# Spreading the next chunk's leaf work over leaves 8 to 14 of a chunked recurrence

## The reference, cut to what matters

```
def step(S, t):
    q_t, k_t, v_t, a_t, b_t = t
    y = jnp.einsum('bhvk,bhk->bhv', S, k_t)
    err = y - v_t
    S = a_t[..., None] * S - (b_t[..., None] * err)[..., None] * k_t[:, :, None, :]
    o = jnp.einsum('bhvk,bhk->bhv', S, q_t)
    return (S, o)
...
o = (o - mu) * jax.lax.rsqrt(var + LN_EPS) * ln_g + ln_b
o = (o * g).reshape(b, t, H * D)
return o @ Wo
```

## Time and profile before

| | us |
|---|---|
| median of 3 runs | 3453.39 (3451.27 to 3462.71) |
| the profiled execution, device time | 3461.74 |
| its span in the trace | 3460.0 |
| first L982 of chunk 0, of chunk 18, of chunk 19, of chunk 20 | 681.56, 1975.95, 2048.01, 2122.75 |
| mean granted TensorE clock, share of full speed | 0.933 |

### The profile page before, as it was taken

One profiled execution on the slowest core, in us unless ns is written; L12 is line 12 of the kernel. 1 busy time (PEld: TensorE's weight loads), 2 busy tenths in 40 slices (PEclk: granted clock), 3 DMA queues, 4 the chain that ended last, 5 costly groups with the idle time before them and its releaser, 6 DMA issues. The chain is left out here.

```text
span 3460.0 us, 48170 instructions
## 1 busy us (share of the span) xinstructions
PE 3028.8 (88%) x14200; PEld 2149.0 (62%) x14200; DVE 2450.5 (71%) x4820; ACT 1595.4 (46%) x3478; POOL 1265.9 (37%) x1452
## 2 busy tenths in 40 slices
PE   5999999378889888898888988889898898788888
PEld 3555555266777677776677767777677776534454
DVE  5777777388888878888878888888888878332222
ACT  3666666255455544555445554555545545211110
POOL 1757666333344333443334433334333344200000
PEclk9999999699999999999989999999999999889999
DMA  1655556621132211322113221122211220110000
GB/s 66 247 216 231 232 211 252 172 43 37 37 62 40 50 39 38 59 43 50 39 37 57 45 50 39 38 57 45 49 39 38 57 45 19 36 61 19 18 18 18
DMA packets 431891, 255.04 MB, mean 74 GB/s; under 512 B 400080, under 2 KB 414128, under 8 KB 416944
## 3 DMA queue, kind: packets, MB, share of 16 engines
q1 hardware_dynamic: 431680, 252.42, 26.4%
HBM read 147.40 MB, written 104.99 MB: 73 GB/s over the span
## 5 line engine op out<-in xcount | busy, mean ns | idle before, releaser
L245 DVE SCALAR_TENSOR_TENSOR A_acc<-A_psY,A_w,A_acc 128x410 f32<-128x410 f32 (+1 forms) x720 | 419.3, 637 | 156.0 <-ACT A_acc L285 156.0
L768 POOL TENSOR_TENSOR B_WT<-B_WT,B_G 128x128 f32<-128x128 f32 (+2 forms) x224 | 186.6, 833 | 869.1 <-issue 446.9
L1069 ACT ACTIVATE B_WL<-B_psT 128x128 f32<-128x128 f32 (+2 forms) x480 | 150.1, 313 | 654.1 <-PE B_psT L1478 654.1
L345 PE MATMUL A_psY<-A_xT,A_w 128*128 128x413 f32 (+1 forms) x960 | 347.2, 510 | 9.1 <-PE A_psAG L351 7.7
L202 POOL TENSOR_TENSOR A_outs<-A_outs,A_acc 128x410 f32<-128x410 f32 (+1 forms) x240 | 229.4, 988 | 254.3 <-ACT A_outs L293 254.3
L982 DVE TENSOR_TENSOR B_NC<-B_NC,B_psM 128x256 f32<-128x256 f32 x480 | 200.1, 417 | 152.3 <-PE B_psM L1502 104.6
L345 PEld LDWEIGHTS A_psY<-A_xT,A_w 128*128 128x128 f32 x960 | 180.2, 189 | 165.5 <-issue 164.3
L985 DVE TENSOR_REDUCE B_W<-B_NC 128x64 f32<-128x320 f32 x512 | 248.8, 486 | 17.6
L1502 PE MATMUL B_psM<-B_BD,B_WL 128*128 128x128 f32 x1536 | 247.3, 305 | 9.2
L1502 PEld LDWEIGHTS B_psM<-B_BD,B_WL 128*128 128x128 f32 x1536 | 207.6, 207 | 75.5 <-ACT B_WL L1069 74.9
L285 ACT ACTIVATE A_acc<-A_psY,A_w 128x410 f32<-128x410 f32 (+1 forms) x240 | 166.2, 692 | 163.0 <-PE A_psY L345 161.3
(11 more groups left out here) (194 smaller groups left out, 7171.8 us busy)
## 6 DMA issues: line engine op xcount, KB each, us to landing
scr<-A_outs SPq DMA_DIRECT2D x48, 1024.0 KB, 5.5
B_KQ<-scr SPq DMA_DIRECT2D x96, 512.0 KB, 6.5
scr<-A_outag SPq DMA_DIRECT2D x32, 1024.0 KB, 8.1
A_xc<-nbeta SPq DMA_DIRECT2D x18, 1024.0 KB, 8.5
scr<-A_x SPq DMA_DIRECT2D x16, 1024.0 KB, 7.6
B_A<-scr SPq DMA_DIRECT2D x32, 512.0 KB, 4.5
B_C<-scr SPq DMA_DIRECT2D x32, 512.0 KB, 4.6
B_G<-scr SPq DMA_DIRECT2D x32, 512.0 KB, 4.6
```

Source lines behind the costliest of these rows:

```text
L245: nc.vector.scalar_tensor_tensor(a, y, w[:, s, col:col + 1], a, ALU.mult, ALU.add)\
L345: last = nc.tensor.matmul(psY[p][:, y0:y0 + HALO + t1 - t0], wp[:, p, kt, :], xT[:, kt, t0:t1 + HALO], start=kt == 0, stop=kt == KT - 1)
L768: tt(dst, dst, gr, ALU.mult).then_inc(wsc.sem, 1)
L1069: copy = lambda out, in_: nc.scalar.activation(out, in_, ACT.Copy)
```

## The change

The same instructions are issued in another order; two waits of ACT and DVE move with them. Nothing is computed that was not computed before.

- DVE: `decays(g + 1)` is split, its first instruction (L828) goes to leaf 8, the two others stay at leaf 9; `mask_own` of the next chunk moves from leaf 10 to 9, `mask_gram(g, 5)` from 9 to 10, `row_pairs(nxt)` from 12 to 11, `leaf_solution(nxt, ...)` from leaves 13, 14 and the boundary to 12, 13 and 14, `invert` from 12 to 14, `att_sum` from 14 to 15, behind `decay_state`.
- `leaf_solution` is cut into other parts: the third of its 8 instructions goes from part 1 to part 2, the sixth from part 2 to part 3. This holds for the chunk's own second half too (leaves 6 and 7).
- PE: the order of `leaf_jobs` from leaf 8 on. `own` 9 to 8, `gram 5` 8 to 9, `decay 0, 1` 10 to 9, `kk` 11 to 10, `ktok` 13 to 11, `var` 10 to 12, `decay 2, 3` 14 to 13, `wo 0` 12 to 13, `wo 1` 13 to 14 (behind `rstd`).
- ACT follows: `leaf_keys` 8 to 7, `sort_keys` 11 to 9, `pairs_copy` 12 to 11, `squares` 9 to 11, the `ktok` copies 14 to 12, `deviation` 11 to 13, `att_copy` 13 to 14.

```diff
-            8: [("gram", 5)],
-            9: [] if last else [("own", 0, 0), ("own", 0, 1)],
-            10: (out and [("var", 0)] or []) + [("decay", 0), ("decay", 1)],
-            11: [] if last else [("kk", 0, 0), ("kk", 0, 1)],
-            12: ([] if last else [("gram", 0)]) + (wo and [("wo", 0)] or []),
-            13: [("ktok", 0), ("ktok", 1)] + (wo and [("wo", 1)] or []),
-            14: (out and [("rstd", 0), ("rstd", 1)] or []) + [("decay", 2), ("decay", 3)]}
+            8: ([] if last else [("own", 0, 0), ("own", 0, 1)]),
+            9: [("gram", 5)] + [("decay", 0), ("decay", 1)],
+            10: ([] if last else [("kk", 0, 0), ("kk", 0, 1)]),
+            11: [("ktok", 0), ("ktok", 1)],
+            12: (out and [("var", 0)] or []) + ([] if last else [("gram", 0)]),
+            13: [("decay", 2), ("decay", 3)] + (wo and [("wo", 0)] or []),
+            14: (out and [("rstd", 0), ("rstd", 1)] or []) + (wo and [("wo", 1)] or [])}
...
                     step(0, n[:, :, 12:18:5], x02, many(n[:, :, 7:8], 2), ALU.mult)
+                elif part == 2:
                     step(1, n[:, :, 5:16:5], n[:, :, 5:16:5], TMP[:, :, 0:3], ALU.add)
-                elif part == 2:
...
+                else:
                     step(5, rows23, rows23, tmp2, ALU.add)
-                else:
...
+                    elif j == 8 and more:
+                        decays(g + 1, (0,))
                     elif j == 9:
                         if more:
-                            decays(g + 1)
+                            decays(g + 1, (1,))
+                            mask_own(g + 1, 0, 0)
+                            mask_own(g + 1, 0, 1)
+                    elif j == 10:
                         mask_gram(g, 5)
...
                     elif j == 11:
+                        if more:
+                            row_pairs(nxt)
                         decay_state(g, 0)
                         decay_state(g, 1)
                     elif j == 12:
+                        if more:
+                            leaf_solution(nxt, 1)
+                    elif j == 13:
+                        if more:
+                            leaf_solution(nxt, 2)
+                        if more:
+                            mask_gram(g, 0)
+                    elif j == 14:
+                        if more:
+                            leaf_solution(nxt, 3)
                         if g:
                             invert(g - 1)
...
                         decay_state(g, 2)
                         decay_state(g, 3)
+                        if g % 2 and g >= 3:
+                            att_sum((g - 3) // 2)
...
                     add_state(g, i)
-                if more:
-                    leaf_solution(nxt, 3)
```

More of the change, by code:

```diff
@@ L817, in _, with decays @@
             wait(dve, zeros, 0, NZERO)
-            def decays(g):
+            def decays(g, parts=(0, 1)):
                 s = g % 2
@@ L827, in decays @@
                 a, e = by_leaf_row(A[:, s]), E[:, s]
[L828 to L832, removed]
+                if 0 in parts:
+                    tt(e[:, F_ + 1:B_ + 2:3], a[:, 0:3], a[:, 1:4], ALU.mult).then_inc(dec.sem, 1)
+                if 1 in parts:
+                    wait(dve, dec, g, 1)
+                    tt(e[:, F_ + 2:B_ + 1:4], e[:, F_ + 1:RR_ + 1:3], a[:, 2:4], ALU.mult).then_inc(dec.sem, 1)
+                    wait(dve, dec, g, 2)
+                    tt(e[:, F_ + 3], e[:, F_ + 2], a[:, 3], ALU.mult).then_inc(dec.sem, 1)
             def coefs(h):
@@ L1014, in chunk @@
                         leaf_solution(here, 3)
+                    elif j == 8 and more:
+                        decays(g + 1, (0,))
                     elif j == 9:
                         if more:
-                            decays(g + 1)
+                            decays(g + 1, (1,))
+                            mask_own(g + 1, 0, 0)
+                            mask_own(g + 1, 0, 1)
+                    elif j == 10:
                         mask_gram(g, 5)
-                    elif j == 10 and more:
-                        mask_own(g + 1, 0, 0)
-                        mask_own(g + 1, 0, 1)
                     elif j == 11:
+                        if more:
+                            row_pairs(nxt)
                         decay_state(g, 0)
@@ L1151, in pairs_copy, with key_tokens @@
                 copy(X[:, 0:3:2, :], ps[:, 0:4 * HJ2].rearrange("p (k x) -> p k x", k=4)[:, 0:3:2]).then_inc(nlc.sem, 1)
+            def key_tokens(g, i):
+                ps = take_bank(act, g, "ktok", i)
+                wait(act, stu, g, 0)
+                copy(KTOK[:, 4 * i:4 * i + 4, :].rearrange("p n c -> p (n c)"), ps[:]).then_inc(ktok.sem, 1)
             def contact_copy(g):
@@ L1243, in chunk @@
                         pairs_copy(2 * g + 1)
-                    elif j == 12 and more:
+                    elif j == 11 and more:
                         pairs_copy(2 * g + 2)
@@ L1281, in chunk @@
                         decay_copies(g + 1)
[L1282 to L1288, removed]
+                        leaf_keys(2 * g + 2)
+                    elif j == 8 and g:
+                        centered_copy(g - 1, 1)
+                    elif j == 9 and more:
+                        sort_keys(2 * g + 2)
                     elif j == 10 and more:
                         leaf_diagonals(2 * g + 2)
-                    elif j == 11:
+                    elif j == 11 and g:
+                        squares(g - 1)
+                    elif j == 12:
                         if more:
-                            sort_keys(2 * g + 2)
+                            sort_queries(2 * g + 2)
+                        key_tokens(g, 0)
+                        key_tokens(g, 1)
+                    elif j == 13:
                         if g:
                             deviation(g - 1)
-                    elif j == 12 and more:
-                        sort_queries(2 * g + 2)
                     elif j == 14:
[L1299 to L1302, removed]
                         if more:
                             block_keys(2 * g + 2)
-                    if j == 13 and g % 2 and g >= 3:
+                    if j == 14 and g % 2 and g >= 3:
                         att_copy((g - 3) // 2)
```

## The result

The change made the kernel slower: 3477.06 us median against 3455.26 (16 runs each), ratio 1.0069 with a 95% interval of 1.005 to 1.0088, which is +24 us on 3455 (the medians are 22 apart). The forecast was +16.

The account below looks back on a forecast made before the run. No single engine bounds the recurrence: DVE sets leaf 9, PE's in-order queue leaf 11, PE the boundary, with clock falls. Even chunks −31, odd +46, chunks 0 and 1 +1: +16, so 3469 us median; own range 3445 to 3490, whole 3428 to 3500.

Parts of the forecast that it names:

- The bank wait: Leaf 15, odd chunks: wo 1 takes decay 2's bank, so PE waits for DVE until +3.1; +4.8 us per chunk.
- faster by over 2%: Sign of a wrong bank count: the kernel's gain if L1436 in leaf 15 starts without a wait.
- The clock in leaf 15 of odd chunks: Leaf 15, odd chunks: PE's idle of about 2.1 may bring a clock fall; +1.5 us, bounds 0 and 3.7.
- The clock in leaves 13 and 14 of odd chunks: Leaves 13 and 14, odd chunks: one-column var is little work, so the clock may fall; +1.0 us.
- the faster rival: No clock fall in odd chunks' leaf 15 or at var; clock losses under 1.4 per odd chunk; 3427 us, chance 0.25.
- The gaps in leaves 9 and 10: Leaves 9 and 10: two PE gaps of about 0.8 replace an idle of 2.06; gaps as short leave the clock at 1.00.
- nothing moves: Leaf 15, even chunks: decay 2, 3 leave, but L1516 still waits for the leaf's own copy; change 0.
- Leaf 11: Leaf 11: PE's queue ahead falls from 5.52 to 1.94, leaf about 4.1; mean −3.0 us, bounds −2.3 and −3.6.
- The first rival's premise: Premise of the faster rival: the clock does not fall, and clock losses decide the sign; 3427 us, chance 0.25.
- Gain 0: Chunk boundary, leaf 15: moving DVE's last two L863 to leaf 14 brings nothing, as an idle of 1.63 follows them.
- The rival with all three POOL instructions ahead of L828: Leaf 8: L828 waits for all three POOL instructions, +1.0 in all 31 chunks that have it; 3500 us, chance 0.15.
- The exchange rival: Whole kernel: what is done sooner is paid back leaf by leaf, sum within 10 us; 3453 us, chance 0.15.

Follow-up runs that it names:

- Number 1: The changed kernel with wo 0 ahead of decay 2 and 3 in leaf 13's jobs, so wo 1 takes another bank: 0.9907 of the kernel before, 3421.61 us.
- number 2: The changed kernel with both wo jobs back in leaves 12 and 13 and att_copy in leaf 13: 1.0024 of the kernel before.
- number 9: The changed kernel with wo 0 first, 64-column var, POOL's leaf 8 reordered, fillers in chunks without wo and in leaves 8, 9, 10: 0.9749 of the kernel before.
- number 5: The changed kernel with each matmul of var streaming 64 equal columns in place of one: 1.0006 of the kernel before.
- number 7: The changed kernel with wo 0 first, 64-column var, fillers in chunks without wo, POOL's scale_right(11) behind scale_left(9): 0.9791 of the kernel before.
- Number 4: The changed kernel with filler matmuls ahead of and behind rstd in leaf 14 of chunks without wo: 1.0054 of the kernel before.
- number 10: The kernel before with var over 64 columns and fillers in leaf 9 and, in chunks without wo, leaf 13: 0.9723 of the kernel before.
- number 11: The changed kernel in its own PE and POOL order, with var over 64 columns and fillers in leaves 8, 9, 10 and 14: 0.9827 of the kernel before.
- number 3: The kernel before with its two DVE boundary instructions cut to one of 128 columns: 0.9946 of the kernel before.
- number 12: The kernel before with fillers in leaves 9 and 13 and var left on one column: 0.9778 of the kernel before.

## Why the prediction was right

The direction and the size were right, +16 forecast and +24 measured, and the mechanism that carried the sign was the one named. That the total came so near is in part luck: two errors of about 15 us cancelled, and the largest gain had the wrong reason. Term by term, in us per chunk, forecast against the table's means:

```
                    even: forecast  measured    odd: forecast  measured
leaves 0 to 5              +0.1      -0.24            0        -0.33
leaves 6 and 7             +0.1      +0.04           +0.1       +0.04
leaf 8                     +1.4      +1.36           +1.4       +1.26
leaf 9                     -1.0      -0.95           -1.0       -0.97
leaf 10                    -0.2      -0.42           -0.2       -0.36
leaf 11                    -3.0      -2.55           -3.0       -2.69
leaves 12 to 14            +0.5      +0.54           -0.5       -0.13
leaf 15                     0        +0.91           +6.3       +5.18
chunk                      -2.1      -1.30           +3.1       +1.99
```

*The bank wait.* The step "PE waits until +3.1, then runs `wo 1`" came out to the tenth: in chunk 19 `wo 1` starts 3.09 after the leaf's start (2115.55 − 2112.46), with an idle of 2.11, and where the clock did not fall leaf 15 is 15.26, against 10.49 + 4.8 = 15.29. Number 1 shows it by taking the wait alone away; number 2 takes the work of `wo 1` out of leaf 15 with it. At full clock the wait is 2.4 of the 2.7 that an odd chunk of the new order costs. The sign given for a miscount, "faster by over 2%" if `wo 1` starts without a wait, was not worked out from any row: without the wait the kernel is 0.9% faster.

*The clock in leaf 15 of odd chunks.* Taken at +1.5, it was 15.69 − 15.26 = 0.4 in the mean. A leaf 15 near 16.7, as in chunk 19, came in 4 of the 14 chunks, not in all: an idle of 2.1 was followed by a fall nearly always in leaf 9 and only at times here. I had transferred one rate to another place.

*The clock in leaves 13 and 14 of odd chunks.* Taken at +1.0, it was about 1.9: leaf 13 is 4.54 against 3.44 where no fall touches it (number 9), leaf 14 is 6.28 against 5.49 (number 5). With the 0.4 above, clock losses in odd chunks pass the 1.4 that the faster rival allowed.

*The gaps in leaves 9 and 10.* The forecast compared gaps of 0.8 with "gaps as short in leaf 3". That reading was wrong: PE is busy for 3.06 of leaf 3's 3.26 and its one gap is 0.20. The new gaps of 0.79 and 1.10 were harmless in most chunks and not in all: fillers in them took the falls that begin in leaves 10 and 11 from 14 to none (numbers 7 and 9).

*The clock in leaf 15 of even chunks.* Taken at 0, it was +0.91. The step that failed is "nothing moves": `rstd` now waits for DVE's `invert` (L909), which the change moved to leaf 14, and behind `rstd`, where the decays stood, PE is idle again. In chunk 18:

```profile
2038.63 1.06 PE L1438 MATMUL B_ring<-ident,B_rdev 128*128 128x128 f32 x8 [0.99 <-DVE B_rdev L909]
2040.33 0.45 PE L1525 MATMUL B_psM<-ident,B_WE 128*128 128x128 f32 x1 [0.63 <-ACT B_WE L1075]
```

Number 4 fills these idles and leaf 15 is 10.48, as it is in number 10: the clock is the whole of it. (The 10.82 of the kernel before had 0.34 of clock in it too.) Over 15 chunks each, this error of +14 nearly cancels that of −16 in leaf 15 of odd chunks.

*Leaf 11.* The size was right and the reason was mostly wrong. The step said that PE's queue ahead of the leaf, 5.52, becomes 1.94. But 5.52 was the queue at 1.2 GHz: number 10 has the same jobs ahead of the leaf at full clock, and its leaf 11 is 4.21, only 0.26 longer than the 3.95 of the new order. So of the 3.49 that chunk 18 saved there (7.44 to 3.95), 3.23 is the clock that no longer falls ahead of `var` or with it, and 0.26 the shorter queue. The sum could not tell the two apart, because both left leaf 11 at about 4. The first rival's premise, that the clock decides, was nearer the truth than its forecast: the falls moved, most of them from leaves 10 and 11 to leaf 13.

*The boundary.* "Gain 0" for the DVE work there holds for leaf 15 (numbers 10 and 11: 10.48 and 10.47). What the forecast missed is that POOL, no longer held by that work, ends sooner, which gives 0.15 to 0.3 in leaf 0: in chunk 19 its last L721 ran until 0.66 after the opening multiply's start before, and ends 2.35 ahead of it now. The forecast had +0.1 there.

*The locks.* The rival with all three POOL instructions ahead of L828 did not happen; leaf 8 is 4.69 in most chunks, as worked out. The stall at leaf 12 did: L865 takes 1.25 there against 0.84 in leaf 6.

The exchange rival was wrong in its sum, 24 against 10, but described what the order does by itself in even chunks: with the clock held they are level (66.99 and 67.12).

What stays open: why the falls in some leaves change with an edit elsewhere (numbers 1 to 4), and what the falls left in leaf 13 of number 9 follow. The runs only show that they do; with one trace of each kernel, some of the shifts can be differences between executions.

The fastest kernel of all is the old order with fillers and wide `var`, 3353.88 us, 2.8% below the kernel before.

## What to carry to other kernels

Before you move a job on an engine that works in order, count the buffers of a shared ring again from the new place: the wait that a move creates is found on paper, to the tenth of a microsecond. Where a stretch runs at the low clock, price every instruction in it at both levels before you call it a queue; reordering may only be a costly way to avoid an idle that a dozen spare matmuls fill. Test an idea with the clock held in both kernels, or a shifted fall will answer in its place.

## What the hardware showed that I had not expected

- A job of 16 records of one-column matmuls, which keeps PE busy for 1.95 and has no idle over 0.3 close ahead of it, is followed by a fall from 2.4 to 1.2 GHz (leaf 11 at 0.72, number 12). With 64 columns it takes 2.00 and the fall is gone (1.00, number 10).
- Matmuls that compute nothing, 13 in leaf 9 and 10 in leaf 13, in time that PE would have been idle, save 3.0 us of an even chunk (71.00 to 68.01, number 12), and 3.9 with wide `var` (67.12, number 10).
- Cutting two DVE instructions from 384 elements of a partition to 3 took them from 0.60 and 1.45 to 0.58 and 1.05 beside POOL, and to 0.16 each where POOL was idle (number 3).
